# Low-rank weight updates of q, k and v: in three row strips of the array in the head, added to the weights in chunk 2

## The chip, the cores and the metric
One core of a Trainium2 chip runs the kernel. The metric is the device time of one execution in microseconds (us). TensorE (PE) multiplies and transposes, VectorE (DVE), ScalarE (ACT) and GpSimd (POOL) do the rest, SyncE (SP) issues transfers. PEld is the weight load of TensorE.

## What is computed
```python
x = L0_attn_x                                     # (2, 1024, 256)
x = x + 0.5 * _L0_ffn_ref(_layernorm(x), ...)     # feed-forward: gated MLP and routed experts
x = x + _L0_attn_ref(_layernorm(x), ...)          # attention, 16 heads
x = x + 0.5 * _L0_ffn_ref(_layernorm(x), ...)     # the same feed-forward weights again

def lora_linear(x, W, b, Bm, Am):                 # used for q, k, v and o; RANK = 16
    out = jnp.einsum('bld,od->blo', x, W) + b
    upd = jnp.einsum('blr,or->blo', jnp.einsum('bld,rd->blr', x, Bm), Am)
    return out + SCALING * upd                    # SCALING = 0.5
```
The kernel does not compute `upd`. It works out the low-rank product of Bm and Am, 256 x 256, adds half of it to W, and multiplies by the sum. For q, k and v this happens inside the first feed-forward block.

## The kernel before
All 2048 tokens go through the first feed-forward block (`ffn_block`, layer 0) in four chunks of 512 (`CHUNKS`). A chunk has 12 units (`UNITS`): eight of the MLP and four of the experts. Unit `u` of the 48 runs as a pipeline whose order is written out by hand for each engine. On PE: the gate product (`product3`, lines 48 to 50, six 512-column products), then the up product of the same shape or, for an expert unit, four transposes of the mixing weights (`turn_mix`, line 720), then the down product of unit u-2 (lines 741 to 745). ACT takes the tanh of the gate (line 873) and rounds the hidden values to their high part (879). DVE forms gated (1112), hidden (1119 or 1124) and hidden_lo (1103). Around these stand the routing of the experts (DVE, ACT and POOL), and the normalisation of later tokens: statistics (1010), variances (108 to 117), rstd on POOL (123), the normalised rows xn (131), their turns on PE (141), their high part on ACT (840) and low part on DVE (1014). Every wide product is done as three products of rounded halves: the weights and x are split into a high and a low part, ACT rounding and POOL or DVE subtracting (239, 245).

The head stands before unit 0: PE folds the routing weights with the keys (776), turns the first four tiles of x (141, `turn(0)` and `turn(1)`), and begins gate(0). ACT first issues two loads (894, 895), then rounds the first weights.

`RawProjections` holds the weights of q, k and v in space that attention uses later (attn_out in the trace). Their nine loads are issued on SP's queue (277, 279, 280). In units 41, 42 and 43, chunk 3 (`LORA_AT`), PE multiplies the two 16-row factors of one projection into a bank of `mix_ps` (287, two products of 256 columns), DVE adds half of it to the weights (294), and one and two units later ACT rounds the sum (300) and POOL subtracts (305). After the block the projections use the parts.

These lines place the update among PE's work:
```python
if first and LORA_AT <= u < LORA_AT + 3:
    i = u - LORA_AT
    if i == 0:
        pe.wait_ge(x_updated, 3 * CT)
    if i == 2:
        pe.wait_ge(raw.whole_done, 1)
    raw.update_on_tensor(pe, i, mix_ps[:, i % 2, :])
```


## Time and profile before
| what | us |
|---|---|
| median of 3 runs | 835.8 (833.98 to 836.37) |
| the profiled execution | 834.09 |
| its span in the trace | 832.3 |
| PE busy | 807.2 |
| DVE busy | 684.2 |
| ACT busy | 472.6 |
| POOL busy | 189.5 |

The span runs from the first to the last instruction of the trace; 1.8 us of the execution lie around it. Products are pipelined and overlap in the rows, so the rate of PE is read from the distance between two starts, not from the length of a row. Brackets behind a row tell how long the engine was idle before it, and what it waited for. Layer 0's block takes the first 220 us or so: chunk 0 until about 75 us, chunk 3 from about 171 us.

### The profile page before, as it was taken

The page shows a single profiled execution, that of the slowest core. Times are in us where ns is not written, and L with a number is a line of the kernel's source. Part 1 is how long each engine was busy: PE and PEld are TensorE (multiplying, and loading weights), DVE is VectorE, ACT ScalarE, POOL GpSimd, SP SyncE. Part 2 cuts the span into 40 slices and gives each one's busy share as a digit, 9 for nine tenths or more (in the row PEclk, how much of TensorE's full clock was granted, in tenths as well). Part 3 has the DMA queues.
Part 4 walks back from the last instruction along what each step waited for, and adds up shares of the span by engine and source line. Part 5 has one row for each costly group of instructions (what it writes and reads, how often), then busy time and mean ns, then how long its engine had stood idle before and what let it go on. Part 6 is the DMA issues. An engine that isn't in the chain of part 4 may idle for free.

```text
span 832.3 us, 14311 instructions
## 1 busy us (share of the span) xinstructions
PE 807.2 (97%) x5424; PEld 516.6 (62%) x5424; DVE 684.2 (82%) x1130; ACT 472.6 (57%) x897; POOL 189.5 (23%) x203
## 2 busy tenths in 40 slices
PE   5989999999999999999999999999999999999997
PEld 4868788887876433333333444443358888888886
DVE  5998798787699999999999988889846977876865
ACT  4444333342442788888888888888863333333322
POOL 2450212021011033333332421143430201120100
PEclk9999999999999999999999999999999999999999
DMA  8110000000050242223333222210000000000000
GB/s 288 41 27 1 0 1 1 1 2 0 1 90 1 40 78 54 40 39 65 65 65 64 41 39 40 57 35 26 15 14 1 1 2 26 0 26 1 1 25 26
DMA packets 19333, 27.87 MB, mean 33 GB/s; under 512 B 4608, under 2 KB 13632, under 8 KB 19264
## 3 DMA queue, kind: packets, MB, share of 16 engines
q1 hardware_dynamic: 18784, 26.40, 14.4%
q8 instruction: 43, 0.70, 0.4%
q10 hardware_dynamic: 480, 0.56, 0.3%
q14 instruction: 26, 0.21, 0.1%
HBM read 12.09 MB, written 2.10 MB: 17 GB/s over the span
## 4 chain that ended last, share of the span: by engine, by line
PE 85%; DVE 8%; ACT 4%; issue 2%; DMA 1%; DVEq 0%; ACTq 0%; POOL 0%
PE front_ps L1654 16%; PE front_ps L1635 13%; PE max_ps L1595 6%; PE ffn_gate_ps L48 5%; PE ffn_gate_ps L50 5%; PE ffn_gate_ps L49 5%; PE ffn_out_ps L741 5%; PE ffn_out_ps L742 5%; PE ffn_out_ps L745 5%; PE ffn_up_ps L48 3%; PE ffn_up_ps L49 3%; PE ffn_up_ps L50 3%; ACT probs L1785 2%; PE ffn_mix_ps L720 2%; DVE ffn_hidden_lo L1103 1%
## 5 line engine op out<-in xcount | busy, mean ns | idle before, releaser
L1865 DVE TENSOR_REDUCE maxima<-max_ps 128x2 f32<-128x1024 f32 x256 | 311.1, 1223 | 29.7 <-PE max_ps L1595 26.9
L1785 ACT ACTIVATE probs<-front_ps 128x512 f32<-128x512 f32 x512 | 277.2, 597 | 39.3 <-PE front_ps L1635 29.5
L873 ACT ACTIVATE ffn_tanh<-ffn_gate_ps 128x512 f32<-128x512 f32 x96 | 57.4, 598 | 227.5 <-PE ffn_gate_ps L50 227.5
L1654 PE MATMUL front_ps<-probs,values 128*32 128x256 f32 x2048 | 163.4, 391 | 4.5 <-ACT mixed_t L1790 4.0
L1112 DVE SCALAR_TENSOR_TENSOR ffn_gated<-ffn_tanh,ffn_gate_ps 128x512 f32<-128x512 f32 x96 | 65.7, 685 | 61.6 <-ACT ffn_tanh L873 61.2
L1654 PEld LDWEIGHTS front_ps<-probs,values 128*32 128x32 f32 x2048 | 40.8, 107 | 95.3 <-issue 55.7
L1635 PE MATMUL front_ps<-q_stack,k_stack 49*128 49x512 f32 x256 | 94.7, 446 | 0.0
L1595 PE MATMUL max_ps<-ffn_xlo,ffn_xhi 48*128 48x512 f32 x256 | 93.8, 447 | 0.0
L1635 PE MATMUL front_ps<-ffn_xhi,ffn_xlo 49*128 49x512 f32 x256 | 91.6, 456 | 0.0
L1535 POOL TENSOR_TENSOR inverse_sum<-turned,minus_one 128x16 f32<-128x16 f32 x15 | 43.7, 2912 | 207.6 <-ACT turned L1797 207.6
L1595 PE MATMUL max_ps<-k_stack,q_stack 48*128 48x512 f32 x256 | 88.2, 455 | 0.6 <-DVE maxima L1865 0.4
L48 PE MATMUL ffn_gate_ps<-ffn_xhi,block 128*128 128x512 f32 x192 | 78.1, 407 | 1.4 <-DVE ffn_xlo L1014 1.4
L741 PE MATMUL ffn_out_ps<-ffn_hidden_hi,block 128*128 128x512 f32 x192 | 78.9, 411 | 0.0
L50 PE MATMUL ffn_gate_ps<-ffn_xlo,block 128*128 128x512 f32 x192 | 76.0, 396 | 0.0
L49 PE MATMUL ffn_gate_ps<-ffn_xhi,block 128*128 128x512 f32 x192 | 75.7, 394 | 0.0
L742 PE MATMUL ffn_out_ps<-ffn_hidden_hi,block 128*128 128x512 f32 x192 | 75.1, 391 | 0.0
L1103 DVE TENSOR_TENSOR ffn_hidden_lo<-ffn_hidden,ffn_hidden_hi 128x512 fp32r<-128x512 f32 x96 | 72.6, 757 | 0.2
L1635 PEld LDWEIGHTS front_ps<-q_stack,k_stack 49*128 49x128 f32 x256 | 39.0, 185 | 47.3 <-ACT probs L1785 43.9
L1635 PEld LDWEIGHTS front_ps<-ffn_xhi,ffn_xlo 49*128 49x128 f32 x256 | 38.1, 184 | 47.1 <-ACT probs L1785 39.0
L956 POOL TENSOR_TENSOR ffn_mix<-ffn_row_exp,ffn_expo 128x512 f32<-128x512 f32 x32 | 34.5, 1099 | 139.7 <-DVE ffn_row_exp L1080 139.7
L879 ACT ACTIVATE ffn_hidden_hi<-ffn_hidden 128x512 fp32r<-128x512 f32 x96 | 59.8, 623 | 3.4 <-DVE ffn_hidden L1124 1.9
L745 PE MATMUL ffn_out_ps<-ffn_hidden_lo,block 128*128 128x512 f32 x192 | 59.6, 391 | 1.4 <-DVE ffn_hidden_lo L1103 1.4
(205 smaller groups left out, 1287.0 us busy)
## 6 DMA issues: line engine op xcount, KB each, us to landing
q_stack<-block SPq DMA_DIRECT2D x48, 64.0 KB, 2.3
ffn_xhi<-block SPq DMA_DIRECT2D x48, 64.0 KB, 2.3
ffn_xlo<-block SPq DMA_DIRECT2D x48, 64.0 KB, 2.3
k_stack<-block SPq DMA_DIRECT2D x42, 64.0 KB, 2.3
x_sb<-in_x SPq DMA_DIRECT2D x3, 512.0 KB, 9.0
out<-x_sb SPq DMA_DIRECT2D x3, 512.0 KB, 2.9
ffn_out_rows<-in_down SPq DMA_DIRECT2D x4, 256.0 KB, 6.2
weights_again<-in_gate SPq DMA_DIRECT2D x2, 512.0 KB, 3.6
```

Source lines behind the costliest of these rows:

```text
L48: pe.matmul(out, w_hi, x_hi, start=(k == 0), stop=False)
L49: pe.matmul(out, w_lo, x_hi, start=False, stop=False)
L50: done = pe.matmul(out, w_hi, x_lo, start=False, stop=(k == last))
L741: pe.matmul(out_ps[:, k, :], weights.late_hi(piece)[:, at], x_hi, start=(m == 0), stop=False)
L742: pe.matmul(out_ps[:, k, :], weights.late_lo(piece)[:, at], x_hi, start=False, stop=False)
L745: out = pe.matmul(out_ps[:, k, :], weights.late_hi(piece)[:, at], x_lo, start=False, stop=(m == UNITS - 1))
L1103: v.tensor_tensor(hidden_lo[:, u % SPLIT_RING, :], hidden[:, u % HIDDEN_RING, :], hidden_hi[:, u % SPLIT_RING, :].bitcast(F32), ALU.subtra ...
L1595: return pe.matmul(max_ps[:, m % 2, j, :], q_stack[s][rows, qt * P:(qt + 1) * P], k_stack[s][rows, half * HALF:(half + 1) * HALF], start=T ...
L1635: pe.matmul(out, k_stack[s][rows, kt * P:(kt + 1) * P], q_stack[s][rows, half * HALF:(half + 1) * HALF], start=True, stop=True).then_inc(r ...
L1654: mm = pe.matmul(mixed_ps[strip:strip + STRIP, at:at + HALF // 2], values[g % SLOTS][:, kt, j, :], probs[:, (g * KEY_TILES + kt) % PROBS, ...
L1785: act.activation(probs[:, tile % PROBS, j, half * HALF:(half + 1) * HALF], score_ps[:, n % RING, :], ACT.Exp, scale=SCORE_SCALE).then_inc( ...
L1865: v.reduce_max(maxima[:, g % 2, m // 2, m % 2, :], max_ps[:, m % 2, :, :], axis=AXIS_X).then_inc(pair_max, 1)
```

## The change
- The two 16-row factors of q, k and v lie on partitions 0, 32 and 64 of the same columns, not all on partition 0. Their six loads are issued on ACT's queue at the start, behind ACT's two own loads; SP keeps the three loads of the weights.
- PE does all six products in the head, after `turn(1)` and before gate(0): q, k, v for the first half of the features, then q, k, v for the second. The results stand in one bank of `gate_ps` and two of `up_ps`, which units 0 and 1 use next.
- ACT copies the three results, scaled, from those banks to SBUF: q before the full parts of the head, k and v after the tanh of unit 0. PE waits for the copies before up(0), gate(1) and up(1).
- POOL adds the copies to the weights in units 27 to 29, chunk 2 (`WHOLE_AT`); ACT rounds in units 28 to 30, POOL subtracts in units 29 to 31.
- The products in units 41 to 43, DVE's sums there, and two waits of PE are gone.

```diff
--- before.py
+++ after.py
@@ class RawProjections @@
     def load(self, sp, dram):
         for p in "qkv":
             sp.dma_start(self.whole[p], dram[f"w{p}_t"].rearrange("(k p) o -> p k o", p=P)
                          ).then_inc(self.raw_in, 16)
-            sp.dma_start(self.lora_b[p], dram[f"lora_b{p}"]).then_inc(self.raw_in, 16)
-            sp.dma_start(self.lora_a[p], dram[f"lora_a{p}_t"]).then_inc(self.raw_in, 16)
...
+            at, rows = 3 * 2 * KT * DIM, slice(i * RANK_ROWS, i * RANK_ROWS + RANK)
+            self.lora_b[p] = flat[rows, at:at + DIM]
+            self.lora_a[p] = flat[rows, at + DIM:at + 2 * DIM]
...
+    def load_ranks(self, act, dram):
+        for p in "qkv":
+            act.dma_start(self.lora_b[p], dram[f"lora_b{p}"]).then_inc(self.ranks_in, 16)
+            act.dma_start(self.lora_a[p], dram[f"lora_a{p}_t"]).then_inc(self.ranks_in, 16)
+
+    def updates_on_tensor(self, pe, banks):
+        pe.wait_ge(self.ranks_in, 3 * 32)
+        for k in range(KT):
+            for p, bank in zip("qkv", banks):
+                update = pe.matmul(bank[:, k * DIM:(k + 1) * DIM], self.lora_b[p][:, k * P:(k + 1) * P],
+                                   self.lora_a[p], start=True, stop=True)
+        update.then_inc(self.update_ready, 1)
+
+    def copy_update_on_scalar(self, act, i, bank):
+        act.wait_ge(self.update_ready, 1)
+        act.activation(self.update["qkv"[i]], by_features(bank), ACT.Copy, scale=LORA_SCALE
+                       ).then_inc(self.update_done, 1)
+
+    def sum_on_gpsimd(self, pool, i):
         p = "qkv"[i]
-        if i == 0:
-            pe.wait_ge(self.raw_in, 3 * 48)
-        for k in range(KT):
-            update = pe.matmul(bank[:, k * DIM:(k + 1) * DIM], self.lora_b[p][:, k * P:(k + 1) * P], self.lora_a[p],
-                               start=True, stop=True)
-        update.then_inc(self.update_ready, 1)
-
-    def sum_on_vector(self, v, i, bank):
-        p = "qkv"[i]
-        v.wait_ge(self.update_ready, i + 1)
-        v.scalar_tensor_tensor(out=self.whole[p], in0=by_features(bank), scalar=LORA_SCALE,
-                               in1=self.whole[p], op0=ALU.mult, op1=ALU.add).then_inc(self.whole_done, 1)
+        pool.wait_ge(self.raw_in, 3 * 16)
+        pool.wait_ge(self.update_done, i + 1)
+        pool.tensor_tensor(self.whole[p], self.whole[p], self.update[p], ALU.add).then_inc(self.whole_done, 1)
...
@@ ffn_block @@
+    update_banks = (space.up_ps[:, 0, :], space.gate_ps[:, 1, :], space.up_ps[:, 1, :])
...
-    LORA_AT = 3 * UNITS + 5
+    WHOLE_AT = 2 * UNITS + 3
...
             if u < 2:
+                if first:
+                    pe.wait_ge(raw.update_done, (1, 3)[u])
                 return
...
-                if first and c == CHUNKS - 1:
-                    pe.wait_ge(raw.whole_done, 3)
...
+            if first and u == 1:
+                pe.wait_ge(raw.update_done, 2)
...
             turn(0)
             turn(1)
+            raw.updates_on_tensor(pe, update_banks)
...
-            if first and LORA_AT <= u < LORA_AT + 3:
-                i = u - LORA_AT
-                if i == 0:
-                    pe.wait_ge(x_updated, 3 * CT)
-                if i == 2:
-                    pe.wait_ge(raw.whole_done, 1)
-                raw.update_on_tensor(pe, i, mix_ps[:, i % 2, :])
...
+            raw.load_ranks(act, dram)
             weights.round_on_scalar(act, "gate0")
...
             high_parts(1)
+            raw.copy_update_on_scalar(act, 0, update_banks[0])
...
             gate_tanh(u)
+            if u == 0 and first:
+                raw.copy_update_on_scalar(act, 1, update_banks[1])
+                raw.copy_update_on_scalar(act, 2, update_banks[2])
...
-            if first and LORA_AT + 1 <= u < LORA_AT + 4:
-                raw.round_on_scalar(act, u - LORA_AT - 1)
+            if first and WHOLE_AT + 1 <= u < WHOLE_AT + 4:
+                raw.round_on_scalar(act, u - WHOLE_AT - 1)
...
-            if first and LORA_AT + 2 <= u < LORA_AT + 5:
-                raw.subtract_on_gpsimd(pool, u - LORA_AT - 2)
+            if first and WHOLE_AT <= u < WHOLE_AT + 3:
+                raw.sum_on_gpsimd(pool, u - WHOLE_AT)
+            if first and WHOLE_AT + 2 <= u < WHOLE_AT + 5:
+                raw.subtract_on_gpsimd(pool, u - WHOLE_AT - 2)
...
-            if first and LORA_AT <= u < LORA_AT + 3:
-                raw.sum_on_vector(v, u - LORA_AT, mix_ps[:, (u - LORA_AT) % 2, :])
```

PE in the head, from the fold to the first product of gate(0), before and after:

```order
L776 MATMUL ffn_gate_ps<-ffn_hidden 128x64 [waits ffn0_keys_in,ffn0_wq_in,ident_done]
L776 MATMUL ffn_gate_ps<-ffn_hidden 128x64 x7
L141 MATMUL ffn_mix_ps<-ident,norm_xn 128x128 [waits norm0_xn_done,ffn0_fold_out]
L141 MATMUL ffn_mix_ps<-ident,norm_xn 128x128 x3
L141 MATMUL ffn_mix_ps<-ident,norm_xn 128x128 [waits norm0_xn_done]
L141 MATMUL ffn_mix_ps<-ident,norm_xn 128x128 x3
L48 MATMUL ffn_gate_ps<-ffn_xhi,block 128x512 [waits ffn_weights_lo_on_vector,norm0_lo_done]
```

```order
L791 MATMUL ffn_gate_ps<-ffn_hidden 128x64 [waits ffn0_keys_in,ffn0_wq_in,ident_done]
L791 MATMUL ffn_gate_ps<-ffn_hidden 128x64 x7
L142 MATMUL ffn_mix_ps<-ident,norm_xn 128x128 [waits norm0_xn_done,ffn0_fold_out]
L142 MATMUL ffn_mix_ps<-ident,norm_xn 128x128 x3
L142 MATMUL ffn_mix_ps<-ident,norm_xn 128x128 [waits norm0_xn_done]
L142 MATMUL ffn_mix_ps<-ident,norm_xn 128x128 x3
L294 MATMUL ffn_up_ps<-attn_out 128x256 [waits proj_ranks_in]
L294 MATMUL ffn_gate_ps<-attn_out 128x256
L294 MATMUL ffn_up_ps<-attn_out 128x256 x2
L294 MATMUL ffn_gate_ps<-attn_out 128x256
L294 MATMUL ffn_up_ps<-attn_out 128x256
L49 MATMUL ffn_gate_ps<-ffn_xhi,block 128x512 [waits ffn_weights_lo_on_vector,norm0_lo_done]
```

The six products (L294) stand between the turns and gate(0), and bring a wait for the rank loads. Rows with the same text are joined, so `x2` is v of the first half and q of the second.

ACT in the head, from its first loads to the tanh of unit 1, before and after:

```order
L894 DMA ffn_hidden<-in_keys 64x2x64
L895 DMA ffn_hidden<-in_retrieval_t 64x2x256
L239 ACT_TABLE_LOAD
L239 ACTIVATE block<-ffn_sums 128x2x512 [waits ffn_gate0_in]
L898 ACTIVATE route_w<-ffn_gate_ps 128x512 [waits ffn0_folded]
L239 ACTIVATE block<-ffn_sums 128x2x512 [waits ffn_up0_in]
L840 ACTIVATE ffn_xhi<-ffn_mix_ps 128x2x256 [waits norm0_turned] x2
L845 ACTIVATE ffn_full<-ffn_mix_ps 128x512 [waits norm0_lo_done] x2
L239 ACTIVATE block<-ffn_out_rows 128x512 [waits ffn_late0_in]
L873 ACTIVATE ffn_tanh<-ffn_gate_ps 128x512 [waits ffn0_gate_ready]
L239 ACTIVATE block<-ffn_mix 128x2x512 [waits ffn_gate1_in]
L873 ACTIVATE ffn_tanh<-ffn_gate_ps 128x512 [waits ffn0_gate_ready]
```

```order
L903 DMA ffn_hidden<-in_keys 64x2x64
L904 DMA ffn_hidden<-in_retrieval_t 64x2x256
L287 DMA attn_out<-in_lora_bq 16x256
L288 DMA attn_out<-in_lora_aq_t 16x256
L287 DMA attn_out<-in_lora_bk 16x256
L288 DMA attn_out<-in_lora_ak_t 16x256
L287 DMA attn_out<-in_lora_bv 16x256
L288 DMA attn_out<-in_lora_av_t 16x256
L240 ACT_TABLE_LOAD
L240 ACTIVATE block<-ffn_sums 128x2x512 [waits ffn_gate0_in]
L908 ACTIVATE route_w<-ffn_gate_ps 128x512 [waits ffn0_folded]
L240 ACTIVATE block<-ffn_sums 128x2x512 [waits ffn_up0_in]
```

```order
L849 ACTIVATE ffn_xhi<-ffn_mix_ps 128x2x256 [waits norm0_turned] x2
L300 ACTIVATE attn_out<-ffn_up_ps 128x512 [waits proj_update_ready]
L854 ACTIVATE ffn_full<-ffn_mix_ps 128x512 [waits norm0_lo_done] x2
L240 ACTIVATE block<-ffn_out_rows 128x512 [waits ffn_late0_in]
L882 ACTIVATE ffn_tanh<-ffn_gate_ps 128x512 [waits ffn0_gate_ready]
L300 ACTIVATE attn_out<-ffn_gate_ps 128x512 [waits proj_update_ready]
L300 ACTIVATE attn_out<-ffn_up_ps 128x512 [waits proj_update_ready]
L240 ACTIVATE block<-ffn_mix 128x2x512 [waits ffn_gate1_in]
L882 ACTIVATE ffn_tanh<-ffn_gate_ps 128x512 [waits ffn0_gate_ready]
```

Six issues (L287, L288) stand ahead of the table load, one copy (L300) behind the two high parts, and two behind the tanh of unit 0.

PE in unit 41, around the first update, before:

```order
L49 MATMUL ffn_up_ps<-ffn_xhi,block 128x512
L50 MATMUL ffn_up_ps<-ffn_xlo,block 128x512
L287 MATMUL ffn_mix_ps<-attn_out 128x256 [waits proj_weights_in,ffn0_x_updated]
L287 MATMUL ffn_mix_ps<-attn_out 128x256
L741 MATMUL ffn_out_ps<-ffn_hidden_hi,block 128x512 [waits ffn0_hidden_hi_done]
L742 MATMUL ffn_out_ps<-ffn_hidden_hi,block 128x512
```

The two L287 rows are gone after the change, here and in units 42 and 43.

POOL behind the last clip of chunk 2's routing, before and after (attn_out is the space of the weights):

```order
L966 TENSOR_TENSOR ffn_mix<-ffn_mix,ffn_outside 128x2 [waits ffn0_ones_set]
L123 TENSOR_TENSOR norm_rstd<-norm_var,minus_half 128x4 [waits norm0_var_done]
L956 TENSOR_TENSOR ffn_mix<-ffn_row_exp,ffn_expo 128x512 [waits ffn0_mix_turned,ffn0_scaled]
L956 TENSOR_TENSOR ffn_mix<-ffn_row_exp,ffn_expo 128x512
L956 TENSOR_TENSOR ffn_mix<-ffn_row_exp,ffn_expo 128x512 [waits ffn0_mix_turned,ffn0_scaled]
```

```order
L980 TENSOR_TENSOR ffn_mix<-ffn_mix,ffn_outside 128x2 [waits ffn0_ones_set]
L307 TENSOR_TENSOR attn_out<-attn_out 128x512 [waits proj_update_done,proj_weights_in]
L124 TENSOR_TENSOR norm_rstd<-norm_var,minus_half 128x4 [waits norm0_var_done]
L307 TENSOR_TENSOR attn_out<-attn_out 128x512 [waits proj_update_done,proj_weights_in] x2
L317 TENSOR_TENSOR wq_lo<-attn_out,wq_hi 128x512 [waits proj_w_hi_done]
L317 TENSOR_TENSOR wk_lo<-attn_out,wk_hi 128x512 [waits proj_w_hi_done]
L317 TENSOR_TENSOR wv_lo<-attn_out,wv_hi 128x512 [waits proj_w_hi_done]
L970 TENSOR_TENSOR ffn_mix<-ffn_row_exp,ffn_expo 128x512 [waits ffn0_mix_turned,ffn0_scaled]
```

Three adds (L307), one of them ahead of the rstd (L124), and the three subtractions (L317) now stand before the mixing weights of chunk 3.

## Rows read from the trace of the kernel before

**Rows 1.** The page: the chain that ended last, share of the span by engine.
```profile
PE 85%; DVE 8%; ACT 4%; issue 2%; DMA 1%; DVEq 0%; ACTq 0%; POOL 0%
```

**Rows 2.** Waits of PE in the whole execution (us, times, longest); DVE in order of time.
```profile
PE ffn_out_ps L745 <- DVE ffn_hidden_lo L1103: 1.4, 1, 1.4
PE ffn_mix_ps L720 <- POOL ffn_mix L966: 2.4, 2, 2.2
...
59.60 0.69 DVE L1124 TENSOR_TENSOR ffn_hidden<-ffn_gated,ffn_mix_ps 128x512 f32<-128x512 f32 x1 [0.79 <-PE ffn_mix_ps L720]
```

**Rows 3.** PE and PEld in order of time, chunk 3: start, us, what.
```profile
188.34 0.39 PE L48 MATMUL ffn_gate_ps<-ffn_xhi,block 128*128 128x512 f32 x1
...
192.42 0.39 PE L48 MATMUL ffn_gate_ps<-ffn_xhi,block 128*128 128x512 f32 x1
...
195.24 1.13 PE L287 MATMUL ffn_mix_ps<-attn_out 16*128 16x256 f32 x4
196.29 0.50 PE L741 MATMUL ffn_out_ps<-ffn_hidden_hi,block 128*128 128x512 f32 x1
...
208.52 0.39 PE L48 MATMUL ffn_gate_ps<-ffn_xhi,block 128*128 128x512 f32 x1
...
195.23 0.72 PEld L287 LDWEIGHTS ffn_mix_ps<-attn_out 16*128 16x128 f32 x4 [0.35 <-issue]
```

**Rows 4.** DVE in order of time, the same units.
```profile
199.98 0.69 DVE L1112 SCALAR_TENSOR_TENSOR ffn_gated<-ffn_tanh,ffn_gate_ps 128x512 f32<-128x512 f32 x1 [2.65 <-ACT ffn_tanh L873]
```

**Rows 5.** PE in order of time, the head.
```profile
11.80 1.97 PE L141 MATMUL ffn_mix_ps<-ident,norm_xn 128*128 128x128 f32 x8 [0.69 <-ACT route_w L898]
15.21 0.79 PE L48 MATMUL ffn_gate_ps<-ffn_xhi,block 128*128 128x512 f32 x1 [1.43 <-DVE ffn_xlo L1014]
...
18.36 0.63 PE L49 MATMUL ffn_up_ps<-ffn_xhi,block 128*128 128x512 f32 x1
18.78 0.47 PE L50 MATMUL ffn_up_ps<-ffn_xlo,block 128*128 128x512 f32 x1
19.10 0.40 PE L48 MATMUL ffn_up_ps<-ffn_xhi,block 128*128 128x512 f32 x1
19.33 0.40 PE L49 MATMUL ffn_up_ps<-ffn_xhi,block 128*128 128x512 f32 x1
```

**Rows 6.** PE in order of time, attention: two 48-row products on different rows.
```profile
253.64 0.49 PE L1595 MATMUL max_ps<-k_stack,q_stack 48*128 48x512 f32 x2
254.07 0.38 PE L1302 MATMUL front_ps<-wv_hi,ffn_xhi 128*128 128x256 f32 x1
```

**Rows 7.** ACT in order of time, the head, and DVE's second hidden product.
```profile
8.25 1.06 ACT L239 ACTIVATE block<-ffn_sums 128x1024 fp32r<-128x1024 f32 x1 [4.68 <-DMA ffn_sums<-in_gate]
...
22.28 0.60 ACT L873 ACTIVATE ffn_tanh<-ffn_gate_ps 128x512 f32<-128x512 f32 x1 [2.57 <-PE ffn_gate_ps L50]
...
23.71 0.69 DVE L1119 TENSOR_TENSOR ffn_hidden<-ffn_gated,ffn_up_ps 128x512 f32<-128x512 f32 x1
```

**Rows 8.** DMA issues of SP's queue in order of time; landing of the L279 loads.
```profile
7.64 1.55 SPq L208 DMA_DIRECT2D ffn_out_rows<-in_down  x1
...
11.34 1.06 SPq L279 DMA_DIRECT2D attn_out<-in_lora_bq  x1
12.45 0.42 SPq L280 DMA_DIRECT2D attn_out<-in_lora_aq_t  x1
...
DMA to landing us min/median/max: 6.0/6.3/7.2
```

**Rows 9.** POOL beside DVE in chunk 3, then chunk 2: DVE and PE.
```profile
206.43 1.29 POOL L305 TENSOR_TENSOR wk_lo<-attn_out,wk_hi 128x512 fp32r<-128x512 f32 x1 [4.08 <-ACT wk_hi L300]
...
206.78 1.49 DVE L1103 TENSOR_TENSOR ffn_hidden_lo<-ffn_hidden,ffn_hidden_hi 128x512 fp32r<-128x512 f32 x1
...
147.38 0.69 DVE L1112 SCALAR_TENSOR_TENSOR ffn_gated<-ffn_tanh,ffn_gate_ps 128x512 f32<-128x512 f32 x1 [0.96 <-ACT ffn_tanh L873]
...
148.82 0.62 PE L745 MATMUL ffn_out_ps<-ffn_hidden_lo,block 128*128 128x512 f32 x2
```

More of the change, by code:

```diff
@@ L33 @@
 LORA_SCALE = 8.0 / RANK
+RANK_ROWS = 32
 SCORE_SCALE = HD ** -0.5
@@ L262, in __init__ @@
         flat = space[:, :, :, :].rearrange("p a j d -> p (a j d)")
-        self.whole, self.lora_b, self.lora_a = {}, {}, {}
+        self.whole, self.update, self.lora_b, self.lora_a = {}, {}, {}, {}
         for i, p in enumerate("qkv"):
-            at = i * (KT + 2) * DIM
+            at = i * 2 * KT * DIM
             self.whole[p] = flat[:, at:at + KT * DIM].rearrange("p (k o) -> p k o", k=KT)
-            self.lora_b[p] = flat[0:RANK, at + KT * DIM:at + (KT + 1) * DIM]
-            self.lora_a[p] = flat[0:RANK, at + (KT + 1) * DIM:at + (KT + 2) * DIM]
+            self.update[p] = flat[:, at + KT * DIM:at + 2 * KT * DIM].rearrange("p (k o) -> p k o", k=KT)
+            at, rows = 3 * 2 * KT * DIM, slice(i * RANK_ROWS, i * RANK_ROWS + RANK)
+            self.lora_b[p] = flat[rows, at:at + DIM]
+            self.lora_a[p] = flat[rows, at + DIM:at + 2 * DIM]
         self.hi = {p: scope.enter_context(nc.sbuf_tensor(f"w{p}_hi", [P, KT, DIM], F32R)) for p in "qkv"}
         self.lo = {p: scope.enter_context(nc.sbuf_tensor(f"w{p}_lo", [P, KT, DIM], F32R)) for p in "qkv"}
-        self.raw_in = sem("proj_weights_in")
-        self.update_ready, self.whole_done = sem("proj_update_ready"), sem("proj_whole_done")
+        self.raw_in, self.ranks_in = sem("proj_weights_in"), sem("proj_ranks_in")
+        self.update_ready, self.update_done = sem("proj_update_ready"), sem("proj_update_done")
+        self.whole_done = sem("proj_whole_done")
         self.hi_done, self.lo_done = sem("proj_w_hi_done"), sem("proj_w_lo_done")
```

1 line of the change is left out of this document (removed).

## The prediction
> **What bounds the kernel now.** I read the page first: PE holds 85% of the chain that ended last, DVE 8% [rows 1]. Then the waits of PE over the whole execution: a dozen places, and none of them in chunk 3, where the three updates now stand. The two that matter lie in chunk 0, where PE waits 1.4 us for DVE (hidden_lo) and 2.2 us for POOL (the clipped mix) [rows 2]. So in chunk 3 the array is the bound, and time taken from it there is time gained. In the head and chunk 0 it is not so simple: PE waits for others between its first pieces, and after about 24 us DVE is busy nearly without a break until it waits 0.79 us for PE at 59.6 [rows 2], so a delay that reaches DVE at unit 1 is carried to the end, and PE's 3.6 us of waiting do not absorb it.
>
> **Removed in chunk 3.** The view is PE in order of time. A unit without an update runs from one first gate product to the next, 188.34 to 192.42, 4.08 us. The three units with an update run from 192.42 to 208.52, 16.10 us in all [rows 3]. 16.10 - 3 x 4.08 = 3.86 us, 1.29 each. Of that the four records of an update start within 1.13 us of row time, and the rest is the change of shape of the product: PE's weight load sits idle 0.35 us before the 16-row group and the next product starts 1.05 us after it, not one slot of 0.23. Is PE still the bound without them? DVE idles before each of its three gated products there, waiting for the tanh, 2.65 us in the middle unit [rows 4], and it loses three sums of 0.68 us as well, so yes. The whole 3.86 us is a gain. Nothing after it waits on a fixed time: the projections' wait for the rounded weights is met earlier than now.
>
> **Added in the head, PE.** The turns begin at 11.80 and end at 13.77, and the first gate product starts at 15.21, a gap of 1.43 us that waits for DVE's xlo [rows 5]. Six 16-row products go into it. Each leaves two records (12 for 6 in chunk 3), and the array is at its lower level here: neighbouring 512-column products start 0.43 us apart up to 18.78 and 0.23 us from 19.10 on, that is 1.2 and 2.4 GHz, whatever the clock row of the page says [rows 5]. A record of 256 columns at full rate takes about 0.22 us (an estimate: 1.13 us less the last record's 0.37 is 0.76 for three starts, the first 0.10 longer), so 0.43 here. Three ways to count:
> One after another, 12 slots, 5.2 us. Perfectly side by side, q, k and v together, 4 slots, 1.7 us. That products on different rows do overlap is shown: two 48x512 products on rows 0 and 64 lie within 0.49 us, and the next product starts 0.43 us after them, where two alone would need 0.45 without any change of shape [rows 6]. I take a middle: records start in the order of the queue, and the second record of q stands on the same rows as its first and so waits for it; k's first record can start beside q's second, and so on. That is one slot per product and one more at the end, 7 slots, 3.0 us. No row shows two-record products side by side, so both ends stay in the range; I take the middle because nothing in the rows shows a record overtaking another.
> From 13.8 us on, 3.0 us, and 0.2 us for the change back of shape (double the 0.10 of [rows 3]): the first gate product at 17.0 instead of 15.21, 1.8 us late. But the rate doubles at about 18.8 us, and I see nothing that moves this. Work pushed over that point takes half the time, so from there on PE is 0.9 us late. With 4 slots it is 0.25 us, with 12 slots gate(0) starts at 19.0, when ten products had already run: 10 x 0.23 = 2.3 us.
>
> The Trainium skill, TensorE: Matmul & The Clock Gate, section on packing small matmuls, gives a packed group the time of one matmul plus some 4 ns a tile, which is the 4-slot case, and says as well that matmuls start and end in program order, which is what my 7 slots rest on. By the first sentence the result would be 832.2 us, by the second, as I read it for two records, 832.9. The same skill's TensorEngine Tiling, section Key Properties, says that changing the tiling mode drains the engine; the extra 0.35 us of idle weight load before the updates [rows 3] agrees with it.
>
> **Added in the head, ACT.** Six DMA issues go behind the two that ACT has, ahead of its table load and of the rounding of gate0. ACT now idles 4.68 us before that rounding at 8.25 [rows 7]. The six small issues on SP's queue take 0.42 to 0.46 us, but the first took 1.06 [rows 8]. 6 x 0.45 = 2.7 us disappears in the 4.68; 6 x 1.06 = 6.4 would be 1.7 us late. The rest of the chain has 0.6 us of room, since route_w ends at 11.75 and the normalised rows are ready before. I take zero. Landing: 6.0 to 7.2 us after issue on SP's queue, behind megabytes. If ACT's last issue ends by 5.0, they are there by 12.2, before PE asks at 13.8. Zero again. On SP the six issues (3.2 us) vanish, behind everything the head needs. The copy of q's update takes 0.6 us after PE's updates; then come the two full parts and late0, 1.8 us, and tanh(0) can start at 17.0 + 0.6 + 1.8 = 19.4. Gate(0) at 17.0 is done at about 19.4 too, so ACT is just not late. The other two copies, 1.2 us, fall in the 2.57 us that ACT idles before tanh(1) [rows 7]. PE's three waits on the copies are met: the first copy is done at 17.6, before up(0); the second at about 20.6, when gate(1) is due at 21.5. DVE receives its second hidden product 0.9 us late (23.71 becomes 24.6) and carries that on.
>
> **Moved to chunk 2.** DVE loses its three sums; POOL gets three adds of two SBUF operands, about 1.3 us each (the subtraction of the same size: 1.29), and the subtractions move forward with them. The first add runs behind the clip, at 145.0, and so rstd comes 1.3 us later; DVE wants it some 8 us after that. What it costs DVE: beside a POOL subtraction DVE's hidden_lo took 1.49 instead of 0.68 [rows 9]. Six POOL operations in units 28 to 31 could hold DVE up six times 0.8 us, 4.9 us; DVE idles before each of its four gated products there, 0.96 us the first [rows 9], 5.6 us in all, and PE asks for the hidden_lo that DVE wrote by 146.4 us only at 148.8 [rows 9]. I take zero, with 1.0 us as the bound. ACT waits in its queue for the first add (until 146.3) with tanh(29) behind it, due 146.75: met.
>
> **Sum.** The profiled execution took 834.09 us (span 832.3, 1.8 us around it). 834.1 - 3.86 + 0.9 = 831.1, a gain of 2.95 us. The median of the runs is 835.8, 1.7 higher than the profiled one; the same gain from there gives **832.9 us**.
>
> **Rivals.**
> 1. Perfect overlap, 4 slots: the loss is 0.25 us, gain 3.6, 832.2 us. For it: the pair of [rows 6]. Against: those are one-record products. Chance 0.17.
> 2. No overlap, 12 slots: the change doesn't do side by side what it says. Loss 2.3 us, and ACT then follows: its copy at 19.6, two full parts, late0, tanh(0) at 21.4, three microseconds late; gate(1) waits for the second copy until 22.6, two late. Say 2.4 us lost: gain 1.4, 834.4 us. Chance 0.13.
> 3. The array's rate rises earlier, because PE is no longer idle from 13.77 to 15.21. Before its present rise it worked without a pause of 0.3 us from 15.21; before that it had the folds and the turns with gaps. If the level changes near 15.5, the loss is gone (the 3.5 us of lower rate from 15.2 to 18.8 are worth 1.8, more than the 0.9), but ACT's copies then bound unit 0 about where it is: gain 3.9, 831.9 us. Chance 0.10.
> 4. Slower: PE waits for the six rank loads. If each issue on ACT takes 1.55 us, as SP's longest did at 7.64 [rows 8], the last ends at 2.3 + 9.3 = 11.6 and lands 7.2 later, at 18.8; the updates end at 22, gate(0) starts 6.8 us late, and the lower rate lasts longer as well. -3.86 + 6.8 = +2.9: 838.7 us. It decides from a landing after 13.8, is even at about 3.9 us of delay, and is measurable from 6.4. Against: the ACT queue holds only 160 KB. Chance 0.06.
> 5. Small things in one direction or the other: POOL and DVE meeting in chunk 2 (up to 1.0), the drop of the clock around 60 us falling differently. Chance 0.04.
> My own case: 0.50.
>
> **How the numbers follow.** A measurement of this kernel can tell about 0.3%, 2.5 us, from no change; the three runs shown differ by 2.4 us. My case lies just beyond it: faster in 0.6 of it, 0.30. Rival 1 gives 0.13, rival 3 0.08, rivals 2 and 5 together 0.03: faster 0.54. Slower by over 0.3%: rival 4 and a remnant, 0.07. Within: 0.39. The range must hold cases 1, 2, 3 and mine with the scatter of a median: from 831.9 less 1.2 to 834.4 plus 1.2, 830.7 to 835.6.
>
> **What would show it.** In the trace after: 12 records of 16 rows between the turns and gate(0), whose first and last start tell 4, 7 or 12 slots; gate(0) at 17.0; the landing of the last rank load before 13.8; the step from 0.43 to 0.23 us at 18.8 or elsewhere; DVE's second hidden product at 24.6; PE's two waits at 56 and 58 us unchanged in length; three units of 4.08 us where 5.37 stood; no PE wait in units 28 to 33. Wrong would be: updates waiting for loads, tanh(0) later than gate(0) by over a microsecond, or a PE wait in chunk 2.

## The result, and the profile after
The changed kernel takes 830.24 us, median of six runs (828.93 to 832.18), beside 834.79 us (832.92 to 836.37) for the kernel before in the same comparison. The ratio is 0.9949, with a 95% interval of 0.9936 to 0.9963: faster by 4.5 us, half a per cent. The direction was forecast, the size was not: 832.9 us was expected, and 830.24 lies 0.5 us below the range.

The profiled execution of the changed kernel took 832.18 us (span 830.4), the slowest of its six; that of before 834.09 (span 832.3). So the two traces differ by only 1.9 us where the medians differ by 4.5, and where the other 2.6 us are is part of the question.

PE after the change, in order of time, in the head: start, duration, engine and line, product, and in brackets the idle time before it.

```profile
12.45 1.97 PE L142 MATMUL ffn_mix_ps<-ident,norm_xn 128*128 128x128 f32 x8 [0.69 <-ACT route_w L908]
14.35 0.79 PE L294 MATMUL ffn_up_ps<-attn_out 16*128 16x256 f32 x1
14.35 0.79 PE L294 MATMUL ffn_gate_ps<-attn_out 16*128 16x256 f32 x1
14.36 1.21 PE L294 MATMUL ffn_up_ps<-attn_out 16*128 16x256 f32 x2
14.94 0.63 PE L294 MATMUL ffn_gate_ps<-attn_out 16*128 16x256 f32 x1
...
15.37 0.63 PE L294 MATMUL ffn_gate_ps<-attn_out 16*128 16x256 f32 x1
...
15.79 0.63 PE L294 MATMUL ffn_gate_ps<-attn_out 16*128 16x256 f32 x1
15.80 0.63 PE L294 MATMUL ffn_up_ps<-attn_out 16*128 16x256 f32 x1
16.36 0.80 PE L49 MATMUL ffn_gate_ps<-ffn_xhi,block 128*128 128x512 f32 x1
...
20.37 0.63 PE L49 MATMUL ffn_up_ps<-ffn_xhi,block 128*128 128x512 f32 x1
20.80 0.50 PE L50 MATMUL ffn_up_ps<-ffn_xhi,block 128*128 128x512 f32 x1
21.13 0.40 PE L51 MATMUL ffn_up_ps<-ffn_xlo,block 128*128 128x512 f32 x1
```

The twelve records stand in four groups, at 14.35, 14.94, 15.37 and 15.79: three at a time, 0.42 to 0.59 us apart. This is the four-slot case (a slot is the time of one record). The rows start later than in [rows 5] for two reasons that must be kept apart. The folds began at 8.12 here and at 7.47 before, since a load landed later; the first gate product follows the start of the folds by 8.24 us here and by 7.74 before. So the six products cost 0.50 us at this point. Wide products start 0.43 us apart until 20.80 and 0.24 apart from 21.13; before, until 18.78 and from 19.10 [rows 5]. This doubling of the rate is called the step below.

PE in chunk 3, the first gate products that answer to [rows 3]:

```profile
190.70 0.39 PE L49 MATMUL ffn_gate_ps<-ffn_xhi,block 128*128 128x512 f32 x1
...
194.78 0.39 PE L49 MATMUL ffn_gate_ps<-ffn_xhi,block 128*128 128x512 f32 x1
...
207.02 0.39 PE L49 MATMUL ffn_gate_ps<-ffn_xhi,block 128*128 128x512 f32 x1
```

Units 41 to 43 are units of 4.08 us like unit 40: 190.70 to 194.78, and three of them to 207.02. The distance from the first gate product of unit 36 to that of unit 44 fell from 37.42 to 33.56 us, by 3.86.

The waits of PE that answer to [rows 2] (us, times, longest), from the waits of the whole execution:

```profile
PE ffn_mix_ps L735 <- POOL ffn_mix L980: 2.4, 2, 2.2
PE ffn_out_ps L760 <- DVE ffn_hidden_lo L1119: 1.4, 1, 1.4
```

They are unchanged, and no wait stands in units 28 to 33. ACT and its queue in the head, with DVE's second hidden product, answering to [rows 7] and [rows 8]:

```profile
4.33 1.45 ACTq L287 DMA_DIRECT2D attn_out<-in_lora_bv  x1
5.81 1.19 ACTq L288 DMA_DIRECT2D attn_out<-in_lora_av_t  x1
7.02 1.28 ACT L240 ACT_TABLE_LOAD   x1 [7.02 <-issue]
8.92 1.06 ACT L240 ACTIVATE block<-ffn_sums 128x1024 fp32r<-128x1024 f32 x1 [0.61 <-DMA ffn_sums<-in_gate]
...
16.49 0.60 ACT L300 ACTIVATE attn_out<-ffn_up_ps 128x512 f32<-128x512 f32 x1 [1.44 <-PE ffn_up_ps L294]
16.98 1.08 ACT L854 ACTIVATE ffn_full<-ffn_mix_ps 128x512 f32<-128x512 f32 x2
17.93 0.64 ACT L240 ACTIVATE block<-ffn_out_rows 128x512 fp32r<-128x512 f32 x1
19.33 0.60 ACT L882 ACTIVATE ffn_tanh<-ffn_gate_ps 128x512 f32<-128x512 f32 x1 [0.75 <-PE ffn_gate_ps L51]
...
25.41 0.69 DVE L1135 TENSOR_TENSOR ffn_hidden<-ffn_gated,ffn_up_ps 128x512 f32<-128x512 f32 x1
```

The six issues take 4.56 us (four of 0.43 to 0.61, two of 1.45 and 1.19) and leave ACT 0.61 of its 4.68 us of idle time. The loads landed 4.9 to 6.8 us after their issues, the last by 12.2, two microseconds before PE reached the updates. DVE's second hidden product starts at 25.41 instead of 23.71, 1.7 us later: 0.65 of it is the later fold, 0.50 the updates, and the rest goes with the later step. Chunk 2, POOL with the adds, and the DVE instruction beside the first of them:

```profile
147.35 1.28 POOL L307 TENSOR_TENSOR attn_out<-attn_out 128x512 f32<-128x512 f32 x1
148.60 1.47 POOL L124 TENSOR_TENSOR norm_rstd<-norm_var,minus_half 128x4 f32<-128x4 f32 x1
150.04 2.98 POOL L307 TENSOR_TENSOR attn_out<-attn_out 128x512 f32<-128x512 f32 x2
...
148.10 1.10 DVE L1119 TENSOR_TENSOR ffn_hidden_lo<-ffn_hidden,ffn_hidden_hi 128x512 fp32r<-128x512 f32 x1
```

DVE is slowed beside POOL's first add (1.10 us instead of 0.68 before, and 0.72 and 0.85 beside later POOL operations), as [rows 9] let one expect, and PE does not feel it: units 24 to 36 last 47.23 us, and 47.24 before.

### The profile page after: what moved, and what is told of

It reads as the page before. It is cut to its first block, busy times and chain, and to the rows that moved or that the text cites. A ratio compares the mean times of both kernels' runs of the same rounds, so it can differ in the third digit from the quotient of the medians.

```text
span 830.4 us, 14316 instructions
## 1 busy us (share of the span) xinstructions
PE 806.1 (97%) x5424; PEld 516.8 (62%) x5424; DVE 681.9 (82%) x1127; ACT 474.0 (57%) x900; POOL 194.2 (23%) x206
## 4 chain that ended last, share of the span: by engine, by line
PE 85%; DVE 8%; ACT 4%; issue 3%; DMA 1%; DVEq 0%; ACTq 0%; POOL 0%
PE front_ps L1668 17%; PE front_ps L1649 14%; PE max_ps L1609 6%; PE ffn_gate_ps L49 5%; PE ffn_gate_ps L51 5%; PE ffn_gate_ps L50 5%; PE ffn_out_ps L756 5%; PE ffn_out_ps L757 5%; PE ffn_out_ps L760 5%; PE ffn_up_ps L49 3%; PE ffn_up_ps L51 3%; PE ffn_up_ps L50 3%; ACT probs L1799 2%; PE ffn_mix_ps L735 2%; DVE ffn_hidden_lo L1119 1%
```

## The experiments
In this part "landmark" means the start of a unit's first gate product, and "fold" the start of PE's first fold. Times of one batch share the runs of the kernel before: 835.51 us in the first (e1 to e4; 23 runs), 834.47 in the second (e5 to e8; 17 runs, another chip), 835.51 in the third (e9 to e12; 11 runs). Across batches only the ratios are compared, unless a batch is named. A ratio's interval is 1 to 2 us wide to either side, so that costs of half a microsecond are read from the landmarks and not from the medians.

**Does the work in the head cost anything at all?** e1 is the changed kernel without loads, products, copies and adds of the update, so that its q, k and v weights lack their low-rank part; rounding waits for the weights' own loads instead of the adds. e2 is the changed kernel again.

```diff
-            raw.updates_on_tensor(pe, update_banks)
...
-            raw.load_ranks(act, dram)
...
-            raw.copy_update_on_scalar(act, 0, update_banks[0])
...
-                raw.sum_on_gpsimd(pool, u - WHOLE_AT)
```

> The changed kernel without the low-rank updates at all: no rank loads, no six products, no copies, no adds (the q, k and v weights stay without their low-rank part); rounding and subtraction stay in chunk 2. It prices the head. Theory A (what is gained is the 3.86 us of chunk 3, and the head costs something): 3.9 us faster than the kernel before, the changed kernel 0.4 to 1 us slower than this. Theory B (the products in the head pay for themselves, since an array that is busy in that gap gets its full rate earlier): again 3.9 us faster than before, but the changed kernel is as fast or faster than this one.

> The changed kernel once more, beside the others on one chip, with the granted clock of each run. Theory A: 3.4 us faster than before in runs of equal mean clock, and the 4.5 us measured so far hold some scatter of the clock. Theory B: 4.3 us or more faster at equal clock.

Measured: e1 830.95 us, ratio 0.9950 (0.9936 to 0.9965); e2 830.89 us, 0.9952 (0.9938 to 0.9967). The two can't be told apart. The whole low-rank path, six loads, six products, three copies and three adds, costs too little to be seen, 0.06 us between the medians; 0.5 us, as the first gate product tells, is not excluded, and so neither of the two theories is decided by the times. e1 gains 4.6 us on the kernel before, more than the 3.86 of chunk 3, with no update in its head: the surplus does not need the updates. In e1 the rate of PE doubles 5.2 us after gate(0) begins, at 20.6 us, though nothing of the change stands in front of it: a late step as in the changed kernel's trace occurs without the updates as well.

**Do the strips matter?** e3 puts all factors on partitions 0 to 15; e5 keeps the strips and orders the products q, q, k, k, v, v.

```diff
-            at, rows = 3 * 2 * KT * DIM, slice(i * RANK_ROWS, i * RANK_ROWS + RANK)
+            at, rows = (6 * KT * DIM, (6 * KT + 2) * DIM, KT * DIM)[i], slice(0, RANK)
```

```diff
-        for k in range(KT):
-            for p, bank in zip("qkv", banks):
+        for p, bank in zip("qkv", banks):
+            for k in range(KT):
```

> The changed kernel with the factors of all three projections on partitions 0 to 15, so that the six products of the head follow one another. If the side by side placing is what makes the head cheap: the products take 12 slots of 0.43 us, 5.2 us, in place of 4, gate(0) starts 3.4 us later than in the changed kernel, and the time is 1.7 (if the rate rises at the same time) to 3.4 us (if it rises as late after gate(0) as before) longer than the changed kernel's. If the place of the products doesn't matter: equal.

> The changed kernel with the six products of the head in another order: both of q, both of k, both of v, each still on its own strip. If products start strictly in the order of the queue (the step of the prediction that counted 7 slots), a strip's later record holds up the next strip: 10 slots of 0.43 us, gate(0) 2.6 us later than in the changed kernel, 1.3 to 2.6 us longer. If each strip takes its own records on as it comes free: 4 slots, and the time of the changed kernel.

Measured: e3 833.90 us, 0.9986 (0.9974 to 0.9997); e5 830.73 us, 0.9959 (0.9945 to 0.9973). PE in order of time, e3:

```profile
13.71 1.22 PE L294 MATMUL ffn_up_ps<-attn_out 16*128 16x256 f32 x2
14.72 1.06 PE L294 MATMUL ffn_gate_ps<-attn_out 16*128 16x256 f32 x2
...
19.12 0.80 PE L49 MATMUL ffn_gate_ps<-ffn_xhi,block 128*128 128x512 f32 x1
```

and e5:

```profile
13.30 0.79 PE L294 MATMUL ffn_up_ps<-attn_out 16*128 16x256 f32 x1
13.31 0.79 PE L294 MATMUL ffn_gate_ps<-attn_out 16*128 16x256 f32 x1
13.33 1.19 PE L294 MATMUL ffn_up_ps<-attn_out 16*128 16x256 f32 x2
13.90 0.63 PE L294 MATMUL ffn_gate_ps<-attn_out 16*128 16x256 f32 x1
...
15.33 0.80 PE L49 MATMUL ffn_gate_ps<-ffn_xhi,block 128*128 128x512 f32 x1
```

On one strip the same products take twelve slots, 5.41 us from 13.71 to gate(0), where three strips take 2.01 (14.35 to 16.36); gate(0) follows the fold by 11.64 us instead of 8.24, and the kernel loses 3.0 us against e2 of the same batch, most of what chunk 3 gave. In e5 both products of q stand in the queue before the first of k, and yet the records start three at a time, in four slots as before. So a strip with a record in flight does not hold up the next strip, and the order among the strips does not matter. The order of starts shows it too: k's first record (gate_ps, 13.31) starts ahead of three of q's four records, which all precede it in the program. In e3 the rate doubles at 23.0 us, 3.9 after gate(0), although 16-row products had kept PE at work for 5.4 us before. In this trace they did not bring the step forward, and the loss of 3.0 us (3.3 in the landmark of unit 12, beside e2's trace) is close to the whole 3.4 us by which gate(0) is later, not half of it.

**Is it the loads on ACT's queue?** e4 is the kernel before with the six rank loads moved to ACT's queue.

```diff
+            act.dma_start(self.lora_b[p], dram[f"lora_b{p}"]).then_inc(self.raw_in, 16)
+            act.dma_start(self.lora_a[p], dram[f"lora_a{p}_t"]).then_inc(self.raw_in, 16)
```

> The kernel before with one part of the change alone: the six rank loads are issued on ACT's queue behind its own two. If they hold up the load of the routing weights (it landed at 8.12 us after the change, at 7.47 before): the fold starts 0.6 us later and the kernel is 0.3 to 0.6 us slower than before. If that was chance: equal, the fold near 7.5.

Measured: 834.89 us, 0.9998 (0.9986 to 1.0009). The queue change alone shows no effect, within 1.2 us in the one direction and 0.8 in the other. The start of the folds, which waits for a load, is no witness: 6.45 us here, and from 6.46 to 8.12 in the other kernels with and without these loads.

**Side by side where it stood.** e6 is the kernel before, with three strips and all six products in unit 41; DVE sums in units 41 to 43 as before.

```diff
-            if first and LORA_AT <= u < LORA_AT + 3:
...
+            if first and u == LORA_AT:
+                pe.wait_ge(x_updated, 3 * CT)
+                pe.wait_ge(hidden_done, u)
+                raw.updates_on_tensor(pe, lora_banks)
```

> The kernel before with the three strips alone: all six products side by side in unit 41 (two banks of mix_ps, one of up_ps), sums on DVE in units 41 to 43 as before, nothing moved to the head. Side by side in 4 slots of 0.22 us and one change of shape of about 0.4 us cost 1.3 us where the three groups cost 3.86: 2.6 us faster than before, 1.3 us slower than leaving the products out. If the change of place were what counts and not the strips: under 1 us faster than before.

Measured: 832.68 us, 0.9981 (0.9970 to 0.9991). PE in order of time:

```profile
195.16 0.39 PE L51 MATMUL ffn_up_ps<-ffn_xlo,block 128*128 128x512 f32 x1
195.48 0.48 PE L288 MATMUL ffn_up_ps<-attn_out 16*128 16x256 f32 x1
...
196.24 0.38 PE L288 MATMUL ffn_mix_ps<-attn_out 16*128 16x256 f32 x2
196.55 0.50 PE L745 MATMUL ffn_out_ps<-ffn_hidden_hi,block 128*128 128x512 f32 x1
...
208.64 0.63 PE L724 MATMUL ffn_mix_ps<-ident,ffn_mix 128*128 128x128 f32 x4 [0.92 <-DVE attn_out L295]
```

Unit 36 to unit 44 takes 34.86 us, 1.30 more than with no update and 2.56 less than with three groups. At 2.4 GHz the packed group costs as much as a single group did. Then PE waits 0.92 us for DVE's third sum, and the rest of the chunk is 1.1 us longer, which is why 2.6 us were expected and 1.8 came. So packing alone is worth 1.8 us here, and the changed kernel in the order q, q, k, k, v, v (e5, same batch) is 2.0 us faster still: moving the group to the head, and the sums off DVE, is worth about as much again.

**Is idle time in the gap what keeps the rate low?** e7 is e1 with four wide products (128x512) in the gap between turns and gate(0); their result is never read, and like e1 it leaves the low-rank part out.

```diff
+            weights.wait_split(pe, "gate0")
+            for i in range(4):
+                pe.matmul(up_ps[:, 1, :], hi["gate"][:, 0, 0:P], hi["gate"][:, 0, 0:CHUNK], start=True, stop=True)
```

> The changed kernel without the low-rank updates (as in the first run of the study, the weights stay without their low-rank part), but with four products of 128 rows and 512 columns in the head's gap, whose results nobody reads, 1.7 us at the lower rate. It tells what ends the lower rate. If wide products count and 16-row products do not: the step from 0.43 to 0.23 us comes 3.6 to 5.3 us after the filler's start, before 19.3 us, and the time is 0 to 0.9 us shorter than without the filler. If the step keeps to gate(0)'s start: no earlier than 3.6 us after gate(0), and no gain.

Measured: 829.74 us, 0.9943 (0.9931 to 0.9955). PE in order of time:

```profile
13.77 2.06 PE L795 MATMUL ffn_up_ps<-block 128*128 128x512 f32 x4
15.62 0.72 PE L49 MATMUL ffn_gate_ps<-ffn_xhi,block 128*128 128x512 f32 x1
...
18.15 0.40 PE L49 MATMUL ffn_up_ps<-ffn_xhi,block 128*128 128x512 f32 x1
```

The first product at the full rate starts 2.5 us after gate(0), where the traces without wide filler need 3.1 to 6.1, and 4.4 us after the first wide product. So the step stands nearer to gate(0) than in any of them, by 0.6 us at least, as it did not behind 16-row products; this is one trace, and the others scatter over 3 us. In the time it cannot be told apart from e1: the ratios are 0.9943 and 0.9950, with intervals that overlap.

**The updates in another hole.** e8 takes the six products out of the head and puts them into the stall of chunk 0, between the high and the low part of down(6).

```diff
+            if first and u == FT - DOWN_LAG:
+                pe.wait_ge(n.lo_done, 4)
+                pe.wait_ge(rows_out, 4)
+                pe.wait_ge(gated_done, FT)
+                raw.updates_on_tensor(pe, update_banks)
```

> The changed kernel with its six products, still side by side, moved from the head to unit 8, between the high and the low part of down(6), where PE waits 1.4 and 2.2 us for DVE and POOL; copies by ACT at the end of unit 8. If the head's products cost 0.5 us there and nothing in the stall: gate(0) starts 7.74 us after the fold instead of 8.24, the wait of the low part at about 56 us vanishes, and the kernel is 0.3 to 0.5 us faster than the changed one; more (1.7) if the array, busy in the stall, keeps its full rate after it. If ACT's copies hold up the mix: slower.

Measured: 830.12 us, 0.9950 (0.9936 to 0.9963), the same as the changed kernel. Gate(0) follows the fold by 7.74 us, as expected; the gain of 0.3 to 0.5 us is too small for this comparison. The products start at 53.82 to 54.6 us, 0.2 to 0.3 us a slot, and fill PE's wait of 1.4 us for hidden_lo; the wait of 2.18 us for POOL's clip stands as it was, and ends the stall in both kernels.

**Both idle places filled.** e9 is e8 with three wide products in the gap of the head and eight in front of the turns of the mixing weights in unit 8; e10 adds sixteen wide products on a tile of ones at the very start. None of these results is read; the outputs are the full computation.

```diff
+            weights.wait_split(pe, "gate0")
+            fill(3, up_ps[:, 1, :])
...
+            if u == FT and first:
+                pe.wait_ge(hidden_done, FT)
+                fill(8, up_ps[:, 1, :])
```

> A candidate: the updates in the stall of unit 8 as in e8, and wide products whose results nobody reads in the two places where PE idles in chunk 0: three (1.3 us at the lower rate) between the turns and gate(0), eight (1.8 us) before the mix of unit 8 is turned. If an idle array is what costs it the rate: no fall of the granted clock around 60 us, 1.7 us or 3.4 us saved by whether the fall would have lasted one or two of its steps, and the head's rise up to 1.4 us earlier; 826 to 828 us. If not: the time of e8, 830.

> e9 and sixteen wide products on a tile of ones from the start of the kernel, while PE waits for the load of the routing weights (6.9 us at the lower rate). If the rise needs only sustained wide products before it: the fold takes 1.8 us instead of 3.6, gate(0) and up(0) run 0.23 us a product from the start, 2 to 4 us faster than e9. If sixteen take too long they delay the fold by up to 1 us.

Measured: e9 827.29 us, 0.9908 (0.9887 to 0.9929); e10 826.83 us, 0.9901 (0.9883 to 0.9919). Both beat the changed kernel, which took 831.43 us in the same batch (e11, below), by 4.1 and 4.6 us, and the kernel before by 8 us, about 1%. Between e9 and e10 there is no difference that these runs can tell, where 2 to 4 us had been expected of the sixteen products. The stretches of the changed kernel around the stall (stretch, its length, busy us of PE, PEld, DVE, ACT and POOL with counts, mean granted clock, DMA share, GB/s):

```profile
56.00:64.00 8.00, 4.44 (x18) 3.73 (x18) 6.72 (x13) 2.12 (x4) 4.08 (x7) 0.66 0.01 2
64.00:72.00 8.00, 8.00 (x44) 6.78 (x43) 5.64 (x18) 3.48 (x7) 1.01 (x1) 0.91 0.00 0
```

and the same stretches of e9, with rows of its PE in order of time:

```profile
56.00:64.00 8.00, 7.66 (x47) 6.32 (x46) 6.88 (x15) 3.25 (x8) 1.62 (x3) 1.00 0.00 0
64.00:72.00 8.00, 8.00 (x43) 6.74 (x42) 6.40 (x17) 3.75 (x8) 1.01 (x1) 1.00 0.01 2
```

```profile
14.49 0.50 PE L49 MATMUL ffn_gate_ps<-ffn_xhi,block 128*128 128x512 f32 x1
14.83 0.40 PE L50 MATMUL ffn_gate_ps<-ffn_xhi,block 128*128 128x512 f32 x1
...
54.69 2.02 PE L790 MATMUL ffn_up_ps<-block 128*128 128x512 f32 x8
57.05 0.66 PE L735 MATMUL ffn_mix_ps<-ident,ffn_mix 128*128 128x128 f32 x4 [0.34 <-POOL ffn_mix L992]
```

In e9 the granted clock does not fall at 60 us; in the changed kernel its mean over these 8 us is 0.66 (0.79 in the trace of before). Unit 8 to unit 12 takes 20.18 us, against 21.1 to 22.2 in every kernel without the filler: 0.9 us less at least. From the fold to unit 8 e9 takes 42.7 us and e11 44.6, so that the head gives about 1.8 more. In the head the rate doubles with the second gate product. In e10 the folds already run at the high rate (2.00 us of rows instead of 3.65), the turns, after 1.97 us of idle time, run at the low one again, and from 15.32 us the products are 0.23 us apart. So the high rate won by the sixteen products was lost again before gate(0). Which of the two fillers of e9 gives how much of the time was not run apart.

**Once more, both.** e11 is the changed kernel, e12 is e1.

> The changed kernel once more, beside e12, to settle two things with more runs: its level at equal mean clock, and how often the fall of the clock around 60 us lasts twice as long (mean clock 0.995 or 0.996). If the products in the head cost what gate(0)'s later start says: 0.3 to 0.5 us more than e12 at equal clock. If the share of runs with the long fall really depends on the head: about 28%, as in 5 of 18 so far.

> The changed kernel without the low-rank updates once more (the weights stay without their low-rank part). Its head is the one of the kernel before. If the share of the long fall depends on the head: about 55%, as before (22 of 40 runs). If it is chance: anything near the changed kernel's.

Measured: e11 831.43 us, 0.9956 (0.9939 to 0.9973); e12 831.58 us, 0.9951 (0.9932 to 0.9970). Again equal. The long form of the fall, explained below, came in 3 of 5 runs of e11, where about 28% had been expected, and in 4 of 6 of e12.

## Why the prediction was wrong in its size
**The removal, right to the hundredth.** 3.86 us was forecast for chunk 3, and 3.86 us is what the landmarks give in every kernel without the three groups (e1 to e3, e5, e7 to e12). e4, which keeps them, has 37.42 us like before. Behind chunk 3 nothing is lost again: from the last unit of the chunk to the end it is 613.3 us before and 612.9 after.

**Chunk 2, right.** Zero was taken, with 1.0 as the bound. Units 24 to 36 last 47.23 or 47.24 us with and without the adds.

**ACT and the loads, right, with less room than thought.** Two issues of 1.45 and 1.19 us made 4.56 us out of the forecast 2.7; the 4.68 us of idle time just held them. Tanh(0) starts at 19.33, forecast 19.4, but this is luck: the fold began 0.65 us later than in the trace the forecast was made from, gate(0) came at 16.36 and not at 17.0, and ACT had waited 0.75 us for it. The waits for copies and loads cost PE nothing, so rival 4 fell.

**Slots in the head: the step that failed.** The sum's term for the head, +0.9 us, was too large: the six products delay gate(0) by 0.50 us and not by 1.8. The prediction said that records start in the order of the queue and that the second record of q "stands on the same rows as its first and so waits for it", which made seven slots, 3.0 us, and a loss of 0.9. The rows of after show four slots, and e5 shows why: each strip runs through its own records and does not wait for another strip's. The pair in [rows 6] pointed that way and was given too little weight. What the Trainium skill states for a packed group (TensorE: Matmul & The Clock Gate, on packing small matmuls, one matmul's time and some 4 ns a tile) fits the trace, where the three records of a slot start within 0.02 us; its statement that matmuls start in program order, on which the seven slots rested, does not agree with the starts of e5, and here the measurement decides. With four slots the working of the prediction gives 0.25 us, which is rival 1, 832.2 us. That alone would still have been 2.0 us above the result.

**The fixed point at 18.8 us was none.** "I see nothing that moves this", the prediction said of the step from 0.43 to 0.23. The step moves from execution to execution:

| kernel | fold to gate(0) | gate(0) to the double rate | fold to unit 12 |
|---|---|---|---|
| before | 7.74 | 3.9 | 65.25 |
| e4, e6, e1, e12 (nothing ahead of gate(0)) | 7.73 to 7.74 | 5.4, 3.1, 5.2, 6.1 | 66.96, 64.97, 66.69, 67.39 |
| e8 (nothing ahead of gate(0), updates in the stall) | 7.74 | 3.9 | 65.28 |
| after, e2, e11, e5 (four slots) | 8.24 to 8.27 | 4.8, 4.0, 3.8, 3.5 | 66.92, 65.84, 65.69, 65.71 |
| e3 (twelve slots) | 11.64 | 3.9 | 69.19 |
| e7 (wide filler) | 7.81 | 2.5 | 64.68 |
| e9, e10 | 8.03, 7.21 | 0.3, 0.5 | 62.93, 62.09 |

All in us, from PE's rows; the middle column ends at the first product from which the starts stand at the double rate. What follows gate(0) at the low rate was not cut off at a fixed time: e3 begins gate(0) 3.4 us late and sees the step 3.9 us after it, so that it lost 3.0 us in the medians where rival 2 had counted 2.3 to 2.4. Over the whole stretch, the first five traces without work ahead of gate(0) average 66.25 us (66.09 with e8) and the four with it 66.04: the head's cost is inside the scatter. If the step goes along with gate(0), the whole 0.50 us counts and not the half of it, as rival 1 has it; the times can't tell 0.25 from 0.50.

**The median of before was high.** The gain was taken from 835.8, a median of three; the six runs of the comparison gave 834.79. That is 1.0 of the 2.66 us by which the forecast missed; in the batches of the experiments the same kernel gave 835.51, 834.47 and 835.51, so this part is scatter, or the chip. The range had allowed 1.2 for the scatter of one median and none for the other; a forecast made from 834.79 would have had the result inside the range.

**The rest: how often the clock falls long.** Around the stall near 55 to 60 us PE's granted clock is low for a while, and this comes in a shorter and a longer form. The low stretch in the trace of before, and in that of after (columns as above):

```profile
59.91:63.32 3.41, 3.41 (x13) 2.72 (x12) 2.23 (x5) 0.07 (x1) 0.07 (x1) 0.50 0.00 0
58.58:65.38 6.80, 5.00 (x18) 4.50 (x19) 4.33 (x10) 0.38 (x1) 1.61 (x3) 0.50 0.00 0
```

Unit 8 to unit 12 takes 21.1 us (before, e2, e3, e5, e6, e7, e8, e11) or 21.9 to 22.2 (after, e1, e4, e12). The form goes with the step in the head: in the four traces with the long fall the rate doubles 4.8 to 6.1 us after gate(0), in the eight with the short one 2.5 to 4.0. So they are not two separate accidents, and an execution of the long form loses time in both places. What sets the moment of the step was not tried.

A run tells its form, mostly, by its mean granted clock, 0.995 or 0.996 against 0.997 and more. In e6 and e7 this mark fails: three of six runs of e6 at 0.996 have the spans of those at 0.998 (830.5 to 830.9 us), and three runs of e7 at 0.995 and 0.996 are as short as the other two. Spans by that division:

| kernel | runs | at 0.996 or less | mean span | at 0.997 or more | mean span |
|---|---|---|---|---|---|
| before, three batches | 51 | 30 | 833.86 | 21 | 832.05 |
| the changed kernel and e5 | 23 | 8 | 830.16 | 15 | 828.51 |
| e1 and e12 | 12 | 7 | 830.14 | 5 | 827.94 |

Like with like, the change gives 3.7 and 3.5 us (3.7 and 3.3 on the chip of e2 and e11 alone), each uncertain by about 0.5: 3.86 less a loss of 0.2 to 0.4 in the head, where the prediction had 0.9. e1 and e12, with no work in the head, give 3.7 and 4.1. Over all runs the means differ by 4.0 us, and the 0.4 above like with like is the share of long falls, 30 of 51 against 8 of 23, times 1.7. In the six runs of the result it was 2 of 6, and a median of few values between two forms moves further than a mean. So of the miss of 2.66 us, 1.0 is the median of before and some 0.7 the slots. The remaining 1.0 is put down to the forms because nothing else is left; the clock of the six runs of before is not on record, so it is not shown. The forms also explain the two traces: that of before had the short form, that of after the long one, and from the fold to unit 12 the latter takes 1.7 us more. With the later fold (0.65), the 3.86 us of chunk 3 and 0.4 behind it this makes the 1.9 us between their spans.

Whether the change lowers the share is open. With work ahead of gate(0) (the changed kernel, e5, e3) 11 of 35 runs had the long form; without it (before, e4, e1, e12, e8) 45 of 80, e6 and e7 left aside. This speaks for an effect of the head, but the runs are of more than one chip: on that of the second batch before itself had 7 of 17, in the other two batches 23 of 34. 8 of 23 and 7 of 12 alone can be chance. The prediction named this, "the drop of the clock around 60 us falling differently", and gave it 0.04 and no price; its price is 1.7 us at a share of about one half, and the result lies 0.5 us outside the range.

**Rival 3** (the rate rises earlier because the gap is filled) fell in the form it had, a step near 15.5 us: no trace with 16-row products has one before 18.8, and e3, with 5.4 us of them, has it 3.9 us after gate(0). With wide products in the gap the traces of e7 and e9 have it 2.5 and 0.3 us after gate(0). A weaker effect of the 16-row products, on the share of long forms, stays open as said.

## What to carry to other kernels
Small products on three different 32-row strips cost one strip's time here (2.01 us against 5.41), in both orders of the queue that were run: pack them, and put the packed group where PE waits anyway; packing (1.8 us) and place (2.0 us) counted about equally. Before a median is moved by an expected gain, divide its runs by the granted clock and compare within a class. Where PE idles near a fall or a rise of its clock, products whose results nobody reads can be worth more than moving useful narrow ones there: e9 and e10 gained 4.1 and 4.6 us over the changed kernel with eleven and twenty-seven of them, where e8, with the narrow ones alone, gained nothing that could be seen. The narrow ones stood in the wait for hidden_lo and the wide ones in the longer wait for POOL, so that width and place were not tried apart.

## What was not expected of the hardware
- Two-record products on three strips run three at a time also at 2.4 GHz: twelve records with starts 195.48 to 196.24, 0.2 to 0.3 us a slot (e6), and 53.82 to 54.6 (e8).
- Twelve 16-row records over 5.4 us did not bring PE's rate up: it doubled 3.9 us after gate(0) (e3, one trace). Behind four wide products over 1.85 us it doubled 2.5 us after gate(0), 0.6 us or more sooner than in the traces without them (e7, one trace).
- A late step in the head and a long fall of the clock some 38 us later come together: in all four traces with the long fall, and in none of the eight with the short one, the rate doubled later than 4.0 us after gate(0).
- The granted clock reads 1.00 in the head of after from 16.36 to 20.80 us, where wide products start 0.43 us apart, against 0.23 later: 1.2 GHz, and only the spacing tells it.
- Of the six small DMA issues on ACT's queue the first three take 0.43 to 0.61 us in the traces of after, e2 to e5, e8, e9 and e11, the last three 0.44 to 1.55; what makes these long was not tried.
